# New orders of the four engines' lists for the run-up and the last four bodies of a pipelined two-layer kernel

## The reference

```python
def attention_layer(x):                            # x: 16 x 512 x 128, normalised
    q, k, v = split(x @ W_in.T)                    # 16 heads of width 8
    Tq, Tk = cheb(clip(q / sqrt(8))), cheb(clip(k / sqrt(8)))   # beta[0] = 0, so orders 1..5 count
    num = (Tq * cumsum(Tk * v, axis=tokens) * beta).sum(orders)
    den = (Tq.sum(width) * cumsum(Tk.sum(width), axis=tokens) * beta).sum(orders)
    return (num / (den + 1e-7)) @ W_out.T

def transformer_layer(y):
    h = layernorm(y)                               # gains and shifts ln1
    y = y + softmax(causal(q k^T / sqrt(8))) v @ Wp + bp        # q, k, v are projections of h
    h = layernorm(y)                               # gains and shifts ln2
    return y + sum over the top 2 experts e of h @ gate_W + gate_b:
                  w_e * (gelu(h @ W1[e] + b1[e]) @ W2[e] + b2[e])

x = x + attention_layer(layernorm(x))
out = x + transformer_layer(layernorm(x))
```

## Time and profile before

| | |
|---|---|
| median of three runs | 1400.18 us |
| the profiled execution's own time | 1403.43 us |
| its span | 1401.6 us |
| mean granted TensorE clock | 0.906 of full speed |
| busy share PE, DVE, ACT, POOL | 83%, 79%, 67%, 60% |
| run-up, bodies -5 to -1 | 0 to 204.6 us |
| steady bodies 0 to 11 | 204.6 to 933.7 us |
| bodies 12 to 15 | 933.7 to 1089.8 us |
| experts and end | 1089.8 to 1401.6 us |

### The profile page before, as it was taken

One profiled execution on the slowest core, in us unless ns is written; L12 is line 12 of the kernel. 1 busy time (PEld: TensorE's weight loads), 2 busy tenths in 40 slices (PEclk: granted clock), 3 DMA queues, 4 the chain that ended last, 5 costly groups with the idle time before them and its releaser, 6 DMA issues.

```text
span 1401.6 us, 27951 instructions
## 1 busy us (share of the span) xinstructions
PE 1168.8 (83%) x8883; PEld 719.2 (51%) x8883; DVE 1112.8 (79%) x2573; ACT 938.9 (67%) x1859; POOL 838.8 (60%) x1105
## 2 busy tenths in 40 slices
PE   3567899899888898988889888889985899999950
PEld 1234355555544555554455554555534688887740
DVE  4659898979888897979879798867735888888845
ACT  3243578767686776757677686657775788888840
POOL 4776477867676776767667576632314366666660
PEclk8578899989998999989999999879998999999985
DMA  9133032332413223241321323133154122222238
GB/s 213 38 91 76 18 94 68 66 85 59 98 58 75 75 50 88 60 94 58 75 79 39 85 54 88 60 66 96 37 175 165 34 89 70 90 76 79 64 136 359
DMA packets 84436, 121.91 MB, mean 87 GB/s; under 512 B 15270, under 2 KB 66522, under 8 KB 80002
## 3 DMA queue, kind: packets, MB, share of 16 engines
q1 hardware_dynamic: 70978, 98.07, 26.6%
q0 software_dynamic: 9088, 17.33, 3.6%
q10 hardware_dynamic: 4224, 4.72, 1.0%
HBM read 63.96 MB, written 57.46 MB: 87 GB/s over the span
## 4 chain that ended last, share of the span: by engine, by line
PE 59%; DVE 24%; ACT 7%; issue 5%; DMA 2%; another core or an unknown queue 2%; POOL 1%; ACTq 0%; DVEq 0%; SPq 0%; POOLq 0%
DVE nm L634 11%; PE front L1674 8%; PE back L1535 8%; PE back L1686 7%; PE scores L1516 6%; PE maxima L1478 5%; PE front L1403 5%; PE maxima L1480 3%; ACT pr L1054 3%; PE back L1353 3%; PE scores L1518 3%; PE front L1378 2%; DVE front L585 2%; DVE kv L588 2%
## 5 line engine op out<-in xcount | busy, mean ns | idle before, releaser
L634 DVE TENSOR_REDUCE nm<-maxima 128x1 f32<-128x384 f32 (+3 forms) x704 | 422.2, 633 | 103.6 <-PE maxima L1480 83.8
L1054 ACT ACTIVATE pr<-scores 128x384 f32<-128x384 f32 (+1 forms) x768 | 373.2, 523 | 171.4 <-PE scores L1518 123.3
L1478 PE MATMUL maxima<-stack 65*128 65x128 bf16 (+2 forms) x768 | 209.0, 294 | 59.7 <-DVE nm L634 52.3
L1516 PE MATMUL scores<-stack 65*128 65x384 bf16 (+2 forms) x768 | 212.1, 289 | 33.5 <-ACT pr L1054 21.2
L1267 POOL DMA_INDIRECT xg<-rows,sloti x128 | 128.1, 1001 | 120.6 <-ACT rows L1075 44.4
L1535 PE MATMUL back<-pr,vaug 128*9 128x512 f32 (+3 forms) x2048 | 188.9, 473 | 0.3 <-ACT oT L1058 0.2
L1480 PE MATMUL maxima<-stack 128*128 128x128 bf16 x1024 | 188.1, 232 | 1.0 <-DVE nm L634 1.0
L1518 PE MATMUL scores<-stack 128*128 128x128 bf16 x1024 | 184.5, 227 | 0.0
L1516 PEld LDWEIGHTS scores<-stack 65*128 65x128 bf16 x768 | 77.2, 101 | 165.1 <-ACT pr L1054 100.1
L1478 PEld LDWEIGHTS maxima<-stack 65*128 65x128 bf16 x768 | 77.4, 101 | 156.9 <-DVE nm L634 104.8
L1342 POOL DMA_INDIRECT pairs<-xs x104 | 108.2, 1041 | 78.9 <-DVE xs L896 45.0
(11 more groups left out here) (225 smaller groups left out, 2478.8 us busy)
## 6 DMA issues: line engine op xcount, KB each, us to landing
stack<-spread SPq DMA_DIRECT2D x32, 400.0 KB
spread<-qs SPq DMA_DIRECT2D x96, 128.0 KB
spread<-ks SPq DMA_DIRECT2D x96, 128.0 KB
stack<-spread SPq DMA_DIRECT2D x32, 384.0 KB
xs<-xg SPq DMA_DIRECT2D x39, 272.0 KB
stack<-pairs SPq DMA_DIRECT2D x8, 1024.0 KB
stack<-in_consts SPq DMA_DIRECT2D x4, 1280.0 KB
xg<-xs SPq DMA_DIRECT2D x17, 272.0 KB
```

The source lines that it names most:

```text
L634: v.tensor_reduce(nm[:, h:h + heads, t], ring(n)[:, 0:heads * (t + 1) * P].rearrange("p (h n) -> p h n", h=heads), AX.X, ALU.max, negate=T ...
L1054: a.activation(pr[:, n % PR, 0:width], ringE[n % 2][:, 0:width], ACT.Exp).then_inc(W.exp_ready, 1)
L1478: k.matmul(ring(n)[:, at:at + t * P], qst[p][0:OPEN_ROWS, h, own], kst[p][0:OPEN_ROWS, h, 0:t * P], start=(j == 0), stop=True, skip_group_ ...
L1516: k.matmul(dst[:, at + P:at + T - t * P], kst[p][0:OPEN_ROWS, h, own], qst[p][0:OPEN_ROWS, h, (t + 1) * P:T], start=(t == tiles[0]), stop= ...
```

## The change

There are now ten classes instead of three: one for each run-up body (w = 0 to 4), one for the steady bodies (w = 5) and one for each of the last four (w = 6 to 9). The loop over slots is turned inside out by `slotted`: a place of 183 or more (26 or more on POOL) means that an operation of body t-1 is emitted between the operations of body t. All place numbers are rewritten; `second_weights`, `first_weights` and `fold_bias` get other places, `add_bias` (DVE) and `value_bias` (PE), which follow the first body's list before, get places in it, and ACT no longer waits for `const_ready` and `w_loaded` there. PE has the same 5312 instructions, and SyncE's list is the same.

```diff
-        SLOTS, POOL_SLOTS = 129, 25
+        SLOTS, POOL_SLOTS = 183, 26
-        VALUES_PE = ((10, 18, 26, 35, 51, 56, 79, 91, 99, 110, 115, 122),
-                     (14, 15, 26, 34, 45, 61, 82, 88, 97, 110, 117, 123),
-                     (14, 26, 30, 42, 52, 70, 80, 85, 95, 109, 119, 122))
+        VALUES_PE = ((),
+                     (),
+                     (),
+                     (),
+                     (70, 71, 80, 89, 109, 117, 126, 145, 157, 167, 171, 178),
+                     (15, 16, 26, 35, 46, 62, 83, 89, 98, 111, 118, 124),
+                     (18, 22, 33, 44, 49, 63, 72, 187, 200, 208, 216, 223),
+                     (58, 70, 78, 86, 92, 102, 190, 199, 206, 220, 225, 232),
+                     (64, 67, 73, 80, 183, 190, 194, 202, 205, 210, 218, 219),
+                     ())
...
-        SPLIT_DVE, SPLIT_ACT = (6, 8, 10, 12, 14, 16, 18, 34), (2, 4, 6, 8, 10, 12, 22, 40)
-        FOLD_PE = ((10, 12), (44, 6), (60, E * HC - 18))
+        SPLIT_DVE, SPLIT_ACT = (9, 13, 14, 15, 16, 17, 21, 23), (36, 37, 40, 41, 42, 43, 47, 49)
+        FOLD_PE = ((40, 12), (43, 6), (45, E * HC - 18))
...
+        def stages(t):
+            return (*(t + i if 0 <= t + i < B else None for i in range(6)), (t + 1) % 2, t + 5 if t < 0 else max(5, t - 6))
+
         def pipelined(body):
-
             for t in range(-5, B):
-                body(*(t + i if 0 <= t + i < B else None for i in range(6)), (t + 1) % 2, (t >= 0) + (t >= 12))
+                body(*stages(t))
+
+        def slotted(items, slots):
+            for t in range(-5, B):
+                for n in range(slots):
+                    if t > -5:
+                        items(n + slots, *stages(t - 1))
+                    items(n, *stages(t))
...
-                    if at((14, 8, 23), h):
-                        add_products(h, (0, 1))
-                    if at((11, 9, 5), g):
-                        less_first_part(g, 0)
+                if at((None, 27, 31, 29, 19, 9, None, None, None, None), h):
+                    add_products(h, (0, 1))
+                if at((None, None, 32, 31, 16, 10, 4, None, None, None), g):
+                    less_first_part(g, 0)
...
-                    if at((64, 62, 57), f):
-                        take_v(f, h)
+                if at((184, 190, 196, 197, 79, 64, None, None, None, None), f):
+                    take_v(f, h)
...
-                if f == 0:
-                    act.wait_ge(W.const_ready, 4)
-                    act.wait_ge(W.w_loaded, 16 * 9)
-
-            pipelined(body)
+            def consts_there():
+                act.wait_ge(W.const_ready, 4)
+                act.wait_ge(W.w_loaded, 16 * 9)
...
+                if at((None,) + (None,) * 9, f):
+                    consts_there()
+
+            slotted(items, SLOTS)
```

More of the change, by code:

```diff
@@ L1336, in _ @@
+            slotted(items, POOL_SLOTS)
             for i in range(BLOCKS):
@@ new lines, in items @@
+            def items(n, t, b, m, g, h, f, p, w):
+                at = lambda places, stage: n == places[w] and stage is not None
+                if m is not None and n in MAX_PE[w]:
+                    maximum(m, MAX_PE[w].index(n), 1 - p)
+                if b is not None and n in SCORES_PE[w]:
+                    scores(b, SCORES_PE[w].index(n), p)
+                if b is not None and n in VALUES_PE[w]:
+                    values(b, VALUES_PE[w].index(n))
+                if b is None and t is not None:
+                    for i, (place, many) in enumerate(FOLD_PE):
+                        if n == place:
+                            first = sum(m for _, m in FOLD_PE[:i])
+                            for j in range(first, first + many):
+                                fold_bias(j)
+                if at((None, None, None, None, None, 4, 3, 49, 56, 39), t):
+                    output2(t, h)
+                if at((None, 2, 183, 14, 58, 5, None, None, None, None), h):
+                    head_sums(h, kx, X, W.k_t24, W.k_t35, W.ks_mm, W.x1_ready, h)
+                if at((None, 183, 184, 183, 61, 6, None, None, None, None), h):
+                    head_sums(h, qx, Y, W.q_t24, W.q_t35, W.qs_mm, *((W.x2_ready, t + 1) if t is not None else (W.outT_ready, h)))
+                if at((None, None, None, None, None, 23, 24, 74, 70, 41), t):
+                    turn_x2(t)
+                if at((None, None, None, None, None, 30, 38, 81, 76, 42), t):
+                    gate(t)
+                if at((None, 184, 185, 192, 84, 37, None, None, None, None), h):
+                    denominators(h)
+                if at((None, None, 186, 193, 92, 41, 6, None, None, None), g):
+                    turn_ln(g, h, t)
+                if at((None, 185, 187, 197, 98, 47, None, None, None, None), h):
+                    turn_rden(h)
+                if at((None, None, 188, 200, 106, 51, 58, None, None, None), g):
+                    project_q2(g, h)
+                if at((None, None, 189, 196, 103, 56, 52, None, None, None), g):
+                    project_k2(g)
+                if at((None, None, 190, 203, 113, 59, 195, None, None, None), g):
+                    project_v2(g)
+                if at((None, None, None, None, None, 61, 56, 96, 188, 44), t):
+                    ranks(t)
+                if at((0, 186, 191, 210, 121, 65, None, None, None, None), f):
+                    turn_h(f, h, g)
+                if at((None, None, None, None, 97, 70, 67, 183, 193, None), b):
+                    turn_back(b, 0, t)
+                if at((1, 187, 192, 215, 131, 75, None, None, None, None), f):
+                    project_k(f, h, g)
+                if at((2, 188, 193, 221, 141, 78, None, None, None, None), f):
+                    project_q(f)
+                if at((None, None, None, 216, 135, 81, 68, 189, None, None), m):
+                    turn_maxima(m, b, 0)
+                if at((183, 189, 194, 224, 138, 86, None, None, None, None), f):
+                    project_v(f)
+                if at((None, 190, 195, 230, 152, 93, None, None, None, None), h):
+                    spread_rden(h, g, f)
+                if at((None, None, None, None, 133, 102, 204, 195, 197, None), b):
+                    turn_back(b, 1, t)
+                if at((None, 191, 196, 233, 163, 107, None, None, None, None), h):
+                    output1(h, g, f)
+                if at((None, None, None, None, 175, 114, 221, 229, 213, None), b):
+                    turn_back(b, 2, t)
+                if at((None, None, None, None, 181, 127, 226, 235, 220, None), b):
+                    turn_back(b, 3, t)
+                if at((None, None, None, 242, 182, 128, 227, 236, None, None), m):
+                    turn_maxima(m, b, 1)
+                if at((None, None, None, None, 184, 129, 229, 237, 221, None), b):
+                    turn_y(b)
+                if at((184,) + (None,) * 9, f):
```

423 lines of the change are left out of this document (228 added, 195 removed), and 61 rows, old and new, of tables (EXPS_ACT, MAX_DVE, MAX_PE, SCORES_PE).

## The result

Over 21 runs of each, the changed kernel takes 1403.46 us (median) and the kernel before 1396.21. The ratio is 1.0052, 95% interval 1.0029 to 1.0074: slower by 0.5%, some 7 us, where 0.34% faster was forecast; the time lies outside the range of 1388 to 1402. (The three first runs of the kernel before, with their median of 1400.18, lay 4 us above its 21; on the scale of these the forecast is 1391.4, so it is 12 us off.) PE executes 8883 matmuls in either profile. The profiled execution has a span of 1406.6 us at a granted clock of 0.902 (before 1401.6 at 0.906).

The account below looks back on a forecast made before the run. PE and DVE were taken to set the pace, with holes mainly in the run-up and bodies 12 to 14. Terms -4.8 + 0.3 - 1.5 + 1.2 = -4.8 us gave 1395.4 us on the runs' scale, 0.34% faster; range 1388 to 1402.

Parts of the forecast that it names:

- the one on bodies 12 to 14: Bodies 12 to 14: next batch's work begins beside the last steps, 0.5 us per boundary, -1.5 us; bounds +1 and -5.
- The sentence on the seam: Seam of bodies -2 and -1: turn at most 1.4 us later, first score needs only the first half's DMA; nothing counted.
- the prediction's own sign: Start of body 0: 199.8 us by the sum, 204.6 before; within 1 us of 204.6 would mean wrong.
- The slower rival: Steady bodies: PE's values step ahead of scores 14 stalls ACT, up to 0.84 us a body, 10.1 in all; 1405; chance 0.12.
- The run-up: Bodies before body 0: -0.6 - 0.6 - 1.8 - 1.8 = -4.8 us, from filling holes on PE and DVE.
- the terms of bodies -5 to -3: Run-up: -0.6 from `add_bias` passing `fifth_order`, -0.6 from `take_v` passing a square, -1.8 in body -3.
- the -1.8 of body -3: Body -3: `add_products` fill POOL's 3.96 us hole, so `take_v` starts at 85.94, not 87.72; -1.8 us, bounds 0 and -2.94.
- I leave it out: Body -3: q's projection ahead of k's may bring hT earlier by up to another 0.9 us; not counted.
- The seam's -1.8: Seam of bodies -2 and -1: k's head sums made while DVE still reduces maxima; -1.8 us, bounds 0 and -2.44.
- Body 15: Body 15: +1.1 for oT, -0.9 for L489, +1.0 for weights behind b1p, sum +1.2 us; bounds -1 and +3.
- The long L489: Body 15 on POOL: the 1119 ns L489 (median 200) loses its DVE second-weights neighbour, so -0.92 us is likely.
- The pair behind b1p: Body 15: one `second_weights` pair behind b1p, +0.5 us if idle covers it, +1.4 if not, taken +1.0.

Follow-up runs that it names:

- experiment 8: Experiment 1's kernel with PE's swap in each steady body undone (scores of exponential 14 before the values step): 1391.26 us, ratio 0.9940 to the kernel before.
- experiment 6: Experiment 1's kernel with the five run-up bodies in the order before: 1397.10 us, ratio 0.9977 to the kernel before.
- 5: The changed kernel, late issue kept, with SyncE's large transfers held until the first half of the maxima has landed: 1390.98 us, ratio 0.9957 to the kernel before.
- Experiment 7: Experiment 1's kernel with bodies 12 to 15 in the order before: 1389.79 us, ratio 0.9950 to the kernel before.
- experiment 1: The changed kernel with ACT's `put_maxima` of half 0 back at its old place in bodies -1, 12, 13: 1389.76 us, ratio 0.9971 to the kernel before.
- 2: The changed kernel with `put_maxima` of half 0 in bodies -1, 12, 13 as early as its data allow: 1389.25 us, ratio 0.9963 to the kernel before.
- experiment 9: Experiment 1's kernel with POOL's first two `add_products` in body -3 behind the two `less_first_part` again: 1400.20 us, ratio 0.9937 to the kernel before (1409.4 there).
- experiment 10: Experiment 1's kernel with PE's five head sums of k in body -1 behind the turn of the maxima again: 1401.03 us, ratio 0.9944 to the kernel before.
- experiment 3: The kernel before with only `put_maxima` of half 0 moved behind the last exponential in bodies -1, 12, 13: 1412.88 us, ratio 1.0116 to the kernel before.

## Why the prediction was wrong, point by point

**The step that failed** is the one on bodies 12 to 14, with "I take 0.5 us for each of three boundaries, -1.5": they take 8.9 us more, with 8.4 us in the two waits for the late DMA, and 3.9 more are lost to the same cause in body -1. Its bounds, +1 and -5, had no term for a wait that the new places make. The sentence on the seam said of the first half's DMA that it "is all this score needs, so I count nothing"; it looked at body -2, where that was true, and not at body -1, whose put had been moved past all exponentials. The DMAs that moved steps issue were followed where the argument was about them, and not at every place where the tables move one. The list shows it (place 77 to 184, behind the last score, for which SyncE's copies wait too), and the earlier trace rows held a warning: ACT's own DMA issue at each boundary. By the prediction's own sign body 0 was to start at 199.8; it starts at 210.2, 5.6 us later than before. None of the rivals had this mechanism. The slower rival had the sign, with the wrong place (and a slip: beside the swap its sum has -5.1, not -4.5, which leaves its 1405 as it is): experiment 8 finds nothing at the swap, though ACT's exponential 14 in one steady body of the changed kernel does wait a little:

```profile
342.29 1.09 ACT L1112 ACTIVATE pr<-scores 128x512 f32<-128x512 f32 x2 [0.18 <-PE scores L1576]
```

**The run-up**, -4.8 forecast: 3 to 7 measured (experiment 6 against 5, 7, 8), and experiments 1 and 2 lie at 0.996 to 0.997 of the kernel before, where -0.34% was forecast for the whole. The size was right, its working only partly, so the agreement is in part luck. x1 of batch 1 comes at 91.1 in place of 93.5, 2.4 of the 3.0 us that the terms of bodies -5 to -3 sum to (the 91.7 among the signs has only body -3's 1.8 of them; old orders elsewhere: 94.7 to 95.4). PE's first head sums start at 22.66 in place of 23.55, 0.9 for the 0.6 forecast, but the k sums of batch 1 at 58.35 in place of 58.62: 0.3 of the 1.2 forecast for two bodies, and body -3 gives 2.1 for 1.8 in this pair. And the -1.8 of body -3 was put down to POOL's products, while experiment 9 shows that they gave nothing or cost a little. What gives the gain instead must be among the other moves of body -3. q's projection ahead of k's, the term of which I wrote "I leave it out", fits the trace, as POOL has no hole in experiment 9 either, where the products stand in their old place; that it is this one isn't shown, since none of these moves was undone alone. The seam's -1.8 is 0.6 by the brackets (experiment 10): PE made the head sums after its last maxima and not beside DVE's reductions, because the list has them behind these maxima and each of those waits for DVE. I had asked whether x1 was there, and not what else stood in front.

**Body 15**, +1.2 forecast. oT starts 2.26 us after the start of the first weights that pass it, as worked out:

```profile
1066.02 0.71 ACT L1139 ACTIVATE w_first<-w_raw,col 128x512 fp32r<-128x512 f32 x1
...
1068.28 0.58 ACT L1116 ACTIVATE oT<-back 128x512 f32<-128x512 f32 x1
...
1071.39 0.60 ACT L1120 ACTIVATE hn<-back 128x512 f32<-128x512 f32 x1 [2.54 <-PE back L1411]
```

The long L489 stayed (still one of 1119 ns), so its -0.9 was wrong: it runs at 1081.5 beside an L770 of DVE (second weights) again, as it had run beside an L710 before. The pair behind b1p cost nothing: w_now begins 4.0 us after the slots, 4.2 before. Experiment 7 leaves all of bodies 12 to 15 at zero within the 3 to 4 us that the timing tells.

**Steady bodies**: 725.1 us between the x2 of batches 0 and 12, 729.1 before; in the ten other profiles it is 714.1 to 727.4, with the same lists but for the swap. This spread goes with the granted clock of the stretch: 725.5 to 729.1 us at 0.93, 719.6 to 725.1 at 0.94, 714.5 to 719.3 at 0.95, 714.1 at 0.96. It is why a single pair of profiles can't settle a term of a few us.

## What to carry to other kernels

When an order changes, list every queue entry that moves and, for each, who waits for its landing and which large transfers are released at the same point; here a small DMA behind the last matmul, which also released large copies, landed some 5 us later than with these held back. An idle bracket that a move is to fill must be looked at again with all the other moves made: another one may already have filled it, and then the move only delays what it passes. Where an order gains in sum but has lost somewhere, undo single queue entries before whole bodies: experiment 1 changes three numbers and turns a ratio of 1.0052 into 0.9971, and with them in place experiments 7 to 10 (0.9937 to 0.9950, intervals below 1) are faster than both kernels, by 0.5 to 0.6% against the kernel before.

## What the runs showed that I had not expected

- Two 8 KB transfers took 7.1 to 9.5 us beside 784 KB to 4 MB issued at the same moment, and 1.9, 4.7 and 1.9 us when those were held back.
- At the first scores of batches 1 and 14 a wait of 3 to 6.5 us on PE was followed by some 4 us at 0.50 to 0.56 of the full clock, and no wait by 1.00, so its price is more than its bracket: 12.1 us of brackets went with 16 us of time in experiment 3.
- The run-up's profiles of one order differ by up to 5.4 us (x2 of batch 0 at 204.2 and 209.6, at granted clocks of 0.81 and 0.77) between executions.
